# Reordering the table of fills: half-size value fill in slot 3, batch 0's last values in its own slots, key fills shifted

## The reference

```python
q = _split_heads(query @ Wq.T + bq)              # 16 heads of 16, query: 64 rows
k = _split_heads(bank @ Wk.T + bk)               # bank: 1601 context rows
v = _split_heads(bank @ Wv.T + bv)
scores = jnp.einsum('bhqd,bhkd->bhqk', q / score_scale, k)
attn = jax.nn.softmax(scores, axis=-1)
ctx = jnp.einsum('bhqk,bhkd->bhqd', attn, v)
return ctx @ Wo.T + bo
...
x = x + _L0_xattn_ref(_layernorm(x), ctx_1024, ...)   # mean of the context
x = x + _L0_attn_ref(_layernorm(x), ...)              # self attention, 64 x 64
x = x + _L0_ffn_ref(_layernorm(x), ...)               # routed and shared experts
x = x + _L1_xattn_ref(_layernorm(x), ctx_1024, ...)   # as above
x = x + _L1_attn_ref(_layernorm(x), ...)              # convolution, gated recurrence, MLP
x = x + _L1_ffn_ref(_layernorm(x), ...)               # quantised MLP
```

## Time and profile before

| | us |
|---|---|
| median of 3 runs | 2129.41 |
| lowest and highest | 2120.83, 2133.33 |
| profiled execution | 2133.82 |
| its span, first to last instruction | 2132.0 |

### The profile page before, as it was taken

How to read it: one execution, slowest core, us unless ns; L and a number is a source line. 1 busy time by engine, 2 the same in 40 slices (tenths; PEclk the granted TensorE clock), 3 DMA queues, 4 the chain that set the end, 5 groups by cost and what they waited for, 6 DMA issues and landing times.

```text
span 2132.0 us, 72414 instructions
## 1 busy us (share of the span) xinstructions
PE 1976.3 (93%) x31796; PEld 1590.1 (75%) x31796; DVE 1314.6 (62%) x2276; ACT 1049.9 (49%) x1532; POOL 614.4 (29%) x997
## 2 busy tenths in 40 slices
PE   5798999999999999999999989999999998999987
PEld 4577777777778787787778778787787776778764
DVE  2557656856666566666666576665666666566644
ACT  3455445555455555555555544555544444444441
POOL 3322323323233232323323232332323222122201
PEclk8999999999999999999999999999999999999999
DMA  5533434243333333424333324242342321213122
GB/s 184 182 125 119 145 117 138 102 135 128 121 117 114 122 132 117 146 91 159 112 129 124 123 93 162 77 158 90 120 135 85 119 70 61 77 52 105 49 71 69
DMA packets 124469, 243.90 MB, mean 114 GB/s; under 512 B 13952, under 2 KB 44800, under 8 KB 124160
## 3 DMA queue, kind: packets, MB, share of 16 engines
q1 hardware_dynamic: 123568, 239.23, 34.0%
q10 hardware_dynamic: 592, 0.04, 0.0%
HBM read 235.94 MB, written 3.15 MB: 112 GB/s over the span
## 4 chain that ended last, share of the span: by engine, by line
PE 73%; DVE 12%; ACT 7%; issue 5%; POOL 2%; DMA 0%; SPq 0%; POOLq 0%; DVEq 0%; ACTq 0%
PE M L805 11%; PE M L812 11%; PE SC L1023 9%; PE SC L1046 8%; PE O L1067 7%; PE X L862 5%; ACT probT L1269 4%; DVE mx L1612 4%; PE SC L1039 3%; PE M L862 3%; PE X L1133 2%; PE X L1107 1%; PE M L867 1%; PE X L841 1%; PE M L906 1%
## 5 line engine op out<-in xcount | busy, mean ns | idle before, releaser
L1612 DVE TENSOR_REDUCE mx<-SC 128x4 f32<-128x1600 f32 (+1 forms) x256 | 466.8, 1823 | 145.2 <-PE SC L1023 142.1
L1269 ACT ACTIVATE probT<-SC 128x2048 f32<-128x2048 f32 (+1 forms) x256 | 398.8, 1558 | 165.4 <-PE SC L1046 164.9
L654 POOL TENSOR_TENSOR rowsT<-raw,rowsT 128x384 fp32r<-128x384 f32 (+1 forms) x256 | 279.6, 1113 | 394.4 <-ACT rowsT L1323 394.2
L812 PE MATMUL M<-wvs,rowsT 128*128 128x256 f32 x2496 | 358.6, 293 | 2.3 <-ACT kT L1208 1.4
L805 PE MATMUL M<-rowsT,wks 128*128 128x400 f32 (+1 forms) x1536 | 342.7, 364 | 11.6 <-DVE V L1414 4.8
L1208 ACT ACTIVATE kT<-M,bk 128x400 f32<-128x400 f32 (+1 forms) x256 | 151.5, 593 | 382.8 <-PE M L805 382.4
L805 PEld LDWEIGHTS M<-rowsT,wks 128*128 128x128 f32 x1536 | 271.8, 191 | 86.2 <-issue 64.4
L812 PEld LDWEIGHTS M<-wvs,rowsT 128*128 128x128 f32 x2496 | 315.1, 192 | 22.6 <-issue 2.5
L1414 DVE TENSOR_TENSOR V<-M,bv 128x512 f32<-128x512 f32 (+1 forms) x224 | 145.3, 649 | 278.0 <-PE M L812 269.8
L1023 PE MATMUL SC<-kT,bdq 32*128 32x400 f32 (+1 forms) x2048 | 244.9, 546 | 27.7 <-ACT probT L1269 23.0
L1067 PEld LDWEIGHTS O<-probT,V 128*17 128x17 f32 x13312 | 195.0, 99 | 79.7 <-issue 75.2
(11 more groups left out here) (275 smaller groups left out, 2461.3 us busy)
## 6 DMA issues: line engine op xcount, KB each, us to landing
ring<-in_ws_dram SPq DMA_DIRECT2D x428, 256.0 KB, 4.6
summed<-in_ctx_dram SPq DMA_DIRECT2D x60, 800.5 KB, 4.6
raw<-in_ctx_dram SPq DMA_DIRECT2D x64, 384.0 KB, 4.5
raw<-in_ctx_dram SPq DMA_DIRECT2D x32, 512.0 KB, 4.0
ring<-rounded_scratch SPq DMA_DIRECT2D x64, 256.0 KB, 4.0
raw<-in_ctx_dram SPq DMA_DIRECT2D x32, 321.0 KB, 4.7
out_dram<-x SPq DMA_DIRECT2D x16, 128.0 KB, 2.2
kT<-in_ctx_dram SPq DMA_DIRECT2D x2, 800.5 KB, 8.9
```

The lines of the kernel that those rows point to most:

```text
L654: pool.tensor_tensor(rowsT[1][:, c, at], raw[:, c, at], rowsT[0][:, c, at], ALU.subtract).then_inc(low_ready, 1)
L812: mm = pe.matmul(bank[:, (t - 2 * a) * D:(t - 2 * a + 1) * D], rowsT[xp][:, cc, t * P:(t + 1) * P], wvs[wp][:, cc, :], start=(at == cc == ...
L1269: act.activation(probT[step % 3][0:w, :, 0:len(ts), :].rearrange("p j t q -> p j (t q)"), SC[0:w, :, 0:len(ts) * P], ACT.Exp)\
L1612: dve.tensor_reduce(mx[c][:, :, n], SC[:, :, 0:KCH[n][1]], AX.X, ALU.max).then_inc(max_used, 1)
```

## The change

Only the table changes. `value(6)` goes from slot 2 to slot 3 (the short exponential), the four values of the next batch that stood in slots 3, 5, 6, 7 go to 2, 4, 5, 6. In slot 7 `key(1, 2)` moves from the second part into the first. `key(0, 3)` moves in slot 4 from the first part to the second. `key(1, 0)` moves in even batches from slot 4 to slot 5, beside `key(1, 1)`; in odd batches it was there. The half fill ahead of `maxima` is left in slot 0 alone. Values 4, 5 and 6 of batch 0 leave the prologue (slots -5, -4, -3) for slots 0, 1 and 3 of batch 0. Piece 3 of the rows is split one slot later, and its load issued one slot later. All line numbers behind the table are one lower in the new file.

```diff
-FIRST = [[[value(4)], [value(5)], [value(6)], [value(0)], [key(0, 3)], [value(1)], [value(3)], [value(2)]],
...
-SECOND = [[[key(0, 0)], [key(0, 1)], [], [key(0, 2)], [key(1, 0)], [key(1, 1)], [], [key(1, 2), key(1, 3)]],
...
+FIRST = [[[value(4)], [value(5)], [value(0)], [value(6)], [value(1)], [value(3)], [value(2)], [key(1, 2)]]] * 2
+SECOND = [[[key(0, 0)], [key(0, 1)], [], [key(0, 2)], [key(0, 3)], [key(1, 0), key(1, 1)], [], [key(1, 3)]],
...
-HEADS = {4: key(1, 0), 0: key(0, 0)}
+HEADS = {0: key(0, 0)}
-LOAD_AT = (1, 2, 3, 5)
+LOAD_AT = (1, 2, 3, 6)
...
-        if 0 < batch < B:
+        if (what in OWN or batch) and 0 <= batch < B:
...
-    for piece, at in enumerate((-2, -1, 0, 2)):
+    for piece, at in enumerate((-2, -1, 0, 3)):
```

More of the change, by code:

```diff
@@ L143, in value @@
     return "value", v, 0
-FIRST = [[[value(4)], [value(5)], [value(6)], [value(0)], [key(0, 3)], [value(1)], [value(3)], [value(2)]],
-         [[value(4)], [value(5)], [value(6)], [value(0)], [key(0, 3)], [value(1)], [value(3)], [value(2)]]]
-SECOND = [[[key(0, 0)], [key(0, 1)], [], [key(0, 2)], [key(1, 0)], [key(1, 1)], [], [key(1, 2), key(1, 3)]],
-          [[], [key(0, 0), key(0, 1)], [], [key(0, 2)], [], [key(1, 0), key(1, 1)], [], [key(1, 2), key(1, 3)]]]
-EARLY = {-17: [key(0, 0), key(0, 1)], -16: [key(1, 0), key(1, 1)], -15: [key(0, 2), key(1, 2)], -12: [value(0), value(1)], -9: [key(0, 3)], -8: [key(1, 3)], -7: [value(2)], -6: [value(3)], -5: [value(4)], -4: [value(5)], -3: [value(6)]}
+FIRST = [[[value(4)], [value(5)], [value(0)], [value(6)], [value(1)], [value(3)], [value(2)], [key(1, 2)]]] * 2
+SECOND = [[[key(0, 0)], [key(0, 1)], [], [key(0, 2)], [key(0, 3)], [key(1, 0), key(1, 1)], [], [key(1, 3)]],
+          [[], [key(0, 0), key(0, 1)], [], [key(0, 2)], [key(0, 3)], [key(1, 0), key(1, 1)], [], [key(1, 3)]]]
+EARLY = {-17: [key(0, 0), key(0, 1)], -16: [key(1, 0), key(1, 1)], -15: [key(0, 2), key(1, 2)], -12: [value(0), value(1)], -9: [key(0, 3)], -8: [key(1, 3)], -7: [value(2)], -6: [value(3)]}
 FIRST_WARM = (1, 2, 3, 4)
```

## The result

| | before | after |
|---|---|---|
| median, us (14 runs each) | 2131.29 | 2141.17 |
| ratio after to before, 95% interval | | 1.0049 (1.0032 to 1.0067) |
| profiled execution, us | 2133.82 | 2136.38 |

The changed kernel is slower by 10.4 us by the ratio, and by 9.9 by the medians. The forecast was +5.2, within half a per cent: the sign was right, the size half of what came, and the result lies at the edge of what was called no change. Single executions of 2702.0 and 2255.5 us here, and of 4649.85 and 7094.48 us in the experiments, stand far outside all others and are left out of every ratio and mean. The profiled execution of after is a favourable one, 4.8 us under its median, so that the two profiles differ by 2.6 us only. That the profiles and the medians disagree is the first thing that had to be explained.

A forecast was written before the change was run, and what follows sets the result against it. PE, busy 93% of the span, was taken to bound the kernel, with only its waits movable. Slot gains and losses from -6.4 to +7.4 summed to +5.2 us: 2129.4 + 5.2 = 2134.6, range 2118 to 2149.

The forecast's parts named there:

- PE's 1976 us stay, and the only thing that can move is time in which PE stands: Opening step: no matmul is added or removed, so PE's busy time is fixed and only its waits can change.
- The gates: PE's waits in each slot: before the maxima for an exponential (23.0 us in all), before the next scores for DVE's reduction (22.7).
- the stand behind odd slot 7: With one key fill instead of two, PE stands 0.73 for the reduction in batch 29; +7.4 us in all, the largest term.
- the low part of piece 3: Slower rival: key(0, 3) in slot 4 waits for POOL; margin 1.8 us, 2147 if late by 0.4 in every batch; chance 0.14.
- PE's wait before scores: Sign of being right: PE's total wait for reductions ahead of the scores goes up by 8 to 10 us.
- before maxima by less: Sign of being right: PE's total wait for exponentials ahead of the maxima moves by less than the 8 to 10 before scores.
- the swap: Full for half value fill in slot 2 hides waits, -6.4 us; half for full in slot 3 adds waits, +3.5 us.
- the split pair: key(1, 2) and key(1, 3) cost 0.11 more apart than as a pair in odd batches: +1.1 us.
- ACT in odd slots 7: The next exponential can start about 0.5 earlier, PE's scores come 0.7 earlier, so 0.2 late: +1.2 us.
- the 45.7 us at the two gates: PE's waits for exponentials and reductions together, 2% of the span: the pool out of which reordering cover can win.
- Hidden at no cost: the order of banks has as many close pairs as before: Claim, from both programs' order, that the reordered fills cost nothing through waits for banks.
- The clock rival: The emptier prologue drops PE to half clock; some 5 us lost ahead of the scores, 2140; chance 0.03.

The follow-up runs named there:

- after_again: The changed kernel, unedited, run once more beside the kernel before: ratio 1.0041 (1.0017 to 1.0064).
- before_again: The kernel before, unedited, run as if it were a new kernel: ratio 0.9981 (0.9963 to 1.0000).
- prologue_alone: The kernel before with only batch 0's values 4, 5 and 6 moved out of the prologue into slots 0, 1 and 2: ratio 0.9999.
- odd_pair: The changed kernel with odd slot 7 turned: no fill ahead of the maxima, key(1, 2) and key(1, 3) as a pair behind them; ratio 1.0019 to before.
- open5: The changed kernel with odd slot 5's first fill left open, the key pair behind odd slot 7's maxima, half key(1, 0) earlier in even slot 5; ratios 0.9986, 0.9972.

## Why the prediction was half right

**Sign and size.** +5.2 was forecast and +10.4 came, 9.4 over all executions, of which some 1.5 are at equal clock and 8 are the clock. That the result lies near the forecast is in part luck: a sum too high by 3.7 stands against 8 us that it did not have.

**"PE's 1976 us stay, and the only thing that can move is time in which PE stands": wrong.** This is the step that missed the 8 us. PE's stands did not grow, and its 1976.3 and 1977.9 us of work became 1980.0 and 1988.7 for the same matmuls, at more time at the lower clock.

**The gates: right.** In batches 28 and 29 every shift is met within 0.03 us, and so is the stand behind odd slot 7. No wait in slot 2, one in slot 3, the low part of piece 3 in time (in after and after_again no wait of PE for POOL falls into a slot 4): all as the prediction's last part asks. PE's wait before scores is up by 7.5, a little under the 8 to 10; "before maxima by less" leaves open which way, and came as 5.1 down. The order of the terms is right as well: the odd slot 7 was the largest loss and the swap the largest gain. The terms for the split pair (+1.1) and for ACT in odd slots 7 (+1.2) were tested by no run.

**The sum at equal clock: too high by 3.7.** The swap was undersized, 5.5 instead of 2.9. The plain batches are met exactly; what is off lies in slots 2 and 3 with layer work. There the pool of PE's stands was taken too small: it was the 45.7 us at the two gates, while another 31.0 us of stands are called issue, and the swap took 7 to 8 of these away, of which a part came back as other waits. They differ between executions of one kernel: slot 2 of batch 22 takes 7.98 us in the profile of before and 6.28 in before_again, slot 2 of batch 10 7.98 and 7.58. A margin that is read there once has an error as large as the term.

**"Hidden at no cost: the order of banks has as many close pairs as before": right in sum, wrong in place.** The pairs were counted, but not who drains them. A fill drained by DVE became one drained by ACT, in the one slot where ACT has a table load between the exponential and the drain: +1.46 in four batches, 5.8 us. As much went elsewhere, so that PE's waits for the key drain are 9.7 us before and 9.8 after, by luck and not by the count. What the count hid is that single waits of 1.8 us arose, and behind such waits the clock fell more often. The rows for it stood ahead of the prediction, among them.

**The clock rival: looked for in the wrong place and priced too low.** It had 0.03 and the prologue. Its sign did come, the half clock at 80 and 90 us, but prologue_alone has it too, at the same low time as before in the mean. The 5 us of the rival no run shows: two stretches of 3.4 us at 0.37 are 2.5. Most of the added low time lies in the slots 7 and behind, where new waits of 1.8 us arose. The windows of the first slots in the earlier trace rows said nothing on these. The Trainium skill (TensorE: Matmul & The Clock Gate) tells of such falls behind waits of 3 to 5 us for a DMA (HAM oscillation), and in another kernel behind short idle times between groups of matmuls (A second HAM failure mode: psum-queue depth-cycling). The waits of 1.8 us here are nearer to the second.

**What stays open.** That long waits precede the low stretches is seen in the traces: in after_again five of the six low windows hold a stretch that begins within 1.6 us behind a wait of 2.08, 1.80, 1.82, 1.77 or 1.80. But more than half of such waits pass without one, and no run added long waits and nothing else. The runs resolve low time to 7 us only, so that the shares of the stand and of the bank waits are not parted: odd_pair, without either of the changed kernel's, has 10.3 less (± 7.4), about half of the 21.6. Nor is it known why open5 still has 10 us more low time than the kernel before. It has no more windows with long waits, and in its two traces these windows hold 3.4 us of low time and none, so its excess lies outside them.

## What to carry to other kernels

When work is moved, ask of each moved piece which engine frees what it fills, and what stands ahead of that engine's freeing instruction in the new place. Look at the longest single wait and not only at the sum. When two profiles differ less than two medians, put time against granted clock over all executions before looking for the rest in one trace: here it took the standard deviation within the kernel before from 6.1 us to 2.3 and split the difference of two kernels into its parts. Set span less busy time beside it: where the bounding engine's stands are equal and its busy time is not, its clock is the first suspect. And take the margins of every slot from the trace as a budget: the table made from them came out below both kernels, by 0.34% against the kernel before, when batch 0's values were back in the prologue.

## What the runs showed of the hardware

Stretches at the lower clock, most of them 3.4 to 13.7 us long in the traces, occur all through a kernel whose PE is busy 93% of the time: 15 of them in the profiled execution of the kernel before, 20 in that of the changed one. Many move from execution to execution of one program, and the low time ranges from 42 to 107 us in the kernel before. This spread, at 0.37 us per us, explains most of the differences between its executions (correlation 0.93). PE need not be idle for long: in batch 13 of after_again a wait of 1.82 us, in a window where PE was busy for 14.18 of 16.00 us, was followed by half the clock. Such a fall is more frequent behind a long wait, but not certain: of the windows over odd slots 7, 32 of 78 with a wait of 1.3 us or more had one, and 5 of the 117 others.

A table load of ACT took 1.28 us each time, 33 times in the profile of before, and in 31 of them ACT's next instruction began within 0.1 us. PE's first matmul behind an exponential that it stood for began 0.14 us behind its end in all 49 cases, and the one behind a reduction 0.05 to 0.06.
